# One-hot tables of a graph kernel: four groups of four tiles, one digit each, instead of one operation per digit and block

## What is computed

```python
x = ln(x + segsum(exp(-w)[:, None] * x[dst], src))              # layer 0: summed by src
x = ln(x + mlp(segsum(a32, src), segmax(a32, src), mean, u))    # layer 1: summed by src
x = ln(x + conv2(x, src, dst))                                  # layer 2: two convolutions, summed by dst
x = ln(x + attention(x, src, dst, a16))                         # layer 3: softmax over the edges of a dst
```

## Time and profile before

| | us |
|---|---|
| median of three runs | 9911.04 |
| profiled execution, its own time | 9915.06 |
| its span, first to last instruction | 9913.3 |
| src histogram loop (DVE, PE), with POOL's fetches beside it | 34.8 to 268.5 |
| POOL's last scatter of x | 351.1 |
| ranking, POOL's scatters | 383.6 to 2470.2 |
| everything behind the ranking | 2470.2 to 9913.3 |

### The profile page before, as it was taken

One profiled execution on the slowest core, in us unless ns is written; L12 is line 12 of the kernel. 1 busy time (PEld: TensorE's weight loads), 2 busy tenths in 40 slices (PEclk: granted clock), 3 DMA queues, 4 the chain that ended last, 5 costly groups with the idle time before them and its releaser, 6 DMA issues.

```text
span 9913.3 us, 48663 instructions
## 1 busy us (share of the span) xinstructions
PE 1598.8 (16%) x7747; PEld 1337.3 (13%) x7747; DVE 3662.5 (37%) x13931; ACT 2337.8 (24%) x3414; POOL 6882.5 (69%) x6983
## 2 busy tenths in 40 slices
PE   7544444442001400000000000000001000000000
PEld 6444444442000200000000000000001000000000
DVE  8666666663997411111111111111114222222225
ACT  0344444442000222222221222222220111111110
POOL 7677777777002577777777777777777777777776
PEclk7555555555555555555555555555555555555555
DMA  6445444443775122222221122222221222222221
GB/s 263 120 144 146 139 145 143 141 146 99 274 272 194 46 52 52 54 52 54 52 52 49 50 54 52 54 52 52 54 52 33 56 66 63 65 64 63 66 63 42
DMA packets 573559, 913.41 MB, mean 92 GB/s; under 512 B 335117, under 2 KB 351380, under 8 KB 547976
## 3 DMA queue, kind: packets, MB, share of 16 engines
q1 hardware_dynamic: 349752, 652.54, 19.6%
q0 software_dynamic: 223040, 258.35, 12.2%
q10 hardware_dynamic: 528, 0.15, 0.0%
HBM read 496.53 MB, written 414.02 MB: 92 GB/s over the span
## 4 chain that ended last, share of the span: by engine, by line
POOL 69%; issue 23%; DVE 7%; DMA 1%; PE 0%; ACT 0%; DVEq 0%; POOLq 0%; SPq 0%; ACTq 0%
POOL arena_a L673 45%; POOL by_src L621 16%; POOL arena_a L640 4%; DVE arena_a L1318 2%; DVE arena_a L1323 2%; POOL arena_a L590 1%; POOL x_at_start L600 1%; POOL adst_at_start L654 1%; PE banks L984 0%; DVE cap_blk L1281 0%; DVE cap_blk L1280 0%; DVE arena_b L1404 0%; DVE stat L1400 0%; DVE stat L1406 0%; PE banks L958 0%
## 5 line engine op out<-in xcount | busy, mean ns | idle before, releaser
L673 POOL DMA_INDIRECT arena_a<-table_c,decay x3136 | 2958.7, 943 | 1038.6 <-issue 955.1
L621 POOL DMA_INDIRECT by_src<-arena_b,idx_blk x1568 | 1609.0, 1026 | 506.6 <-issue 476.7
L673 POOL DMA_INDIRECT arena_a<-table_at,decay x1568 | 1489.6, 950 | 477.9 <-issue 477.9
L1530 DVE COPY banks<-arena_a 128x64 f32<-128x64 f32 x194 | 52.7, 271 | 3346.0 <-ACT banks L736 3346.0
L736 ACT ACTIVATE banks<-arena_a 128x1024 f32<-128x1024 f32 x196 | 369.6, 1886 | 2997.9 <-DMA arena_a<-table_c,decay 2997.9
L716 ACT ACTIVATE arena_b<-same_dst 128x1024 f32<-128x1024 f32 (+1 forms) x294 | 312.8, 1064 | 1701.3 <-DVE arena_a L1664 1569.2
L1213 DVE SCALAR_TENSOR_TENSOR arena_a<-arena_a,same_dst 128x64 f32<-128x64 f32 x1567 | 436.5, 279 | 709.5 <-DMA arena_a<-ids_rows 705.9
L932 PE MATMUL banks<-ident,chunk_end 128*64 128x128 f32 (+2 forms) x8 | 2.7, 443 | 3963.1 <-DVEq L1041 3963.1
L821 ACT ACTIVATE arena_b<-arena_a,decay 128x64 f32<-128x64 f32 x1568 | 384.8, 334 | 971.2 <-DMA by_src<-arena_b,idx_blk 864.2
L725 ACT ACTIVATE arena_a<-arena_a 128x1024 f32<-128x1024 f32 (+1 forms) x294 | 598.0, 2034 | 3.9 <-DVE arena_a L1664 2.0
L1215 DVE SCALAR_TENSOR_TENSOR arena_b<-arena_a,src_f,before 128x128 bf16<-128x128 f32 x1568 | 537.8, 343 | 0.0
(11 more groups left out here) (278 smaller groups left out, 4824.3 us busy)
## 6 DMA issues: line engine op xcount, KB each, us to landing
arena_a<-ids_rows SPq DMA_DIRECT2D x98, 1024.0 KB, 8.9
states_src<-arena_a SPq DMA_DIRECT2D x98, 1024.0 KB, 4.8
states_c<-arena_a SPq DMA_DIRECT2D x196, 512.0 KB, 2.6
hrows<-by_src SPq DMA_DIRECT2D x98, 776.0 KB, 6.1
states_at<-arena_a SPq DMA_DIRECT2D x98, 576.0 KB, 3.2
x_at_start<-arena_a SPq DMA_DIRECT2D x7, 7168.0 KB
arena_a<-x_at_start SPq DMA_DIRECT2D x98, 512.0 KB, 6.3
arena_a<-table_c,decay POOLq DMA_INDIRECT x3136, 2.4
```

The lines of the kernel that those rows point to most:

```text
L621: pool.indirect_dma_start(out=by_src, out_offset=AT(ap=idx_blk[r][:, k:k + 1], axis=0), in_=rows[r][:, k, :], in_offset=None)\
L673: pool.indirect_dma_start(out=gb[r][:, k * w:(k + 1) * w], out_offset=None, in_=table[g], in_offset=AT(ap=src_i[:, n * J + k:n * J + k + 1 ...
```

## The change

The two operations that make a block's one-hots, one for each digit, become eight: for each of the four groups of four tiles, one operation for `hi` (392 elements a partition) and one for `lo` (512). That holds for the sixteen tiles of the dst positions, for the histogram loop and for the ranking. In the ranking the order changes too: the groups of block n+1 are no longer made after `positions(n-1)`, but the first three after the selections `stage_b(n-1, 1)`, `(n-1, 2)` and `(n-1, 3)`, and the last after `positions(n-1)`. The wait for `hist_added` moves to the first of them. The number of elements written is the same.

```diff
-            def onehots(o, h, at):
-                v.tensor_tensor(oh_hi[h], in_groups(iota_hi), spread(digits[o, "hi"][:, at], HIGH), ALU.is_equal)
-                return v.tensor_tensor(oh_lo[h], in_groups(iota_lo), spread(digits[o, "lo"][:, at], LOW), ALU.is_equal)
+            def onehots_of_group(h, g, hi, lo):
+                for onehot, table, digit in ((oh_hi[h], iota_hi, hi), (oh_lo[h], iota_lo, lo)):
+                    ins = v.tensor_tensor(onehot[:, g], table, bf(digit[:, g * Q:(g + 1) * Q], table.shape[1]), ALU.is_equal)
+                return ins
+
+            def onehots(o, h, at):
+                for g in range(J // Q):
+                    ins = onehots_of_group(h, g, digits[o, "hi"][:, at], digits[o, "lo"][:, at])
+                return ins
...
-            def onehots_of(n):
...
+            def onehots_of(n, g):
+                at = slice(n * J, (n + 1) * J)
+                ins = onehots_of_group(n % 2, g, digits["src", "hi"][:, at], digits["src", "lo"][:, at])
+                if g == J // Q - 1:
+                    ins.then_inc(s("tile_onehots"), 1)
...
                     if n:
                         stage_b(n - 1, q)
+                    if n + 1 < NBLK and q:
+                        if q == 1:
+                            v.wait_ge(s("hist_added"), n + 1)
+                        onehots_of(n + 1, q - 1)
                 if n:
                     positions(n - 1)
                 if n + 1 < NBLK:
-                    v.wait_ge(s("hist_added"), n + 1)
-                    onehots_of(n + 1)
+                    onehots_of(n + 1, J // Q - 1)
```

More of the change, by code:

```diff
@@ L1190, in _ @@
                 of_nodes(o)
-            def onehots_of(n):
[L1194 to L1197, removed]
+            def onehots_of(n, g):
[3 more added lines that the diff above has]
+                    ins.then_inc(s("tile_onehots"), 1)
             v.wait_ge(s("onehots_used"), 2 * NB)
-            onehots_of(0)
+            for q in range(J // Q):
+                onehots_of(0, q)
             v.wait_ge(s("decay_ready"), 1)
```

## The result

The changed kernel takes 10067.45 us (median; 10058.97 to 10082.26), the kernel before 9912.12 us in the runs beside it: a ratio of 1.0158, 95% interval 1.0145 to 1.0172. It is 155 us slower where 78 us of gain were forecast. The profiled execution has a span of 10080.5 us against 9913.3. Going through the stages as in the earlier trace rows gives the difference of 167 us: the first scatter of the ranking comes 26.6 us later (forecast: 32 earlier), the ranking from its first scatter to the end of its last is 36.2 us shorter (forecast: 45), and 177 us are lost behind the ranking, 175 of them in a stage in which the change does nothing, the pass over the sorted rows on DVE (661 us before, 836 after). The three gather passes behind it are as long as before.

What follows compares the result with a forecast made beforehand. POOL's own work and issue were taken to bound the kernel, its DMAs held up by long one-hots. Startup -34, first block +2.3 and ranking -45 made -77 us: 9834 us, range 9808 to 9894.

Steps and rivals of the forecast that it cites:

- One small operation: DVE's one-hots: 0.277 and 0.340 us for 392 and 512 elements, a pair 0.617, a block 2.47 instead of 2.03.
- The first rival: Every small operation costs its whole duration, 0.80 us a pair; first ranking tile 25 us late, 9894 us; chance 0.11.
- the third: Histogram becomes the bound: small form streams at 1.1 ns an element, a pair 1.09 us; about 10,050 us; chance 0.07.
- the second: The ranking gains nothing, as four pairs catch as much as one block did; 9879 us; chance 0.12.
- the mean wait is the sum of the squared streaming times over twice the pair's time: POOL beside the histogram loop: 0.09 us mean wait, so a fetch costs 1.335 us and a scatter of x 1.37.
- 18 us wait for `node_index` 2: Startup: 49 scatters of x end at 234, `node_index` 2 comes at 252, so POOL waits 18 us, a new wait.
- The ranking: One-hots in eight pieces hold POOL up 16 us where 61 are measured; 45 us saved, range 25 to 61.
- longer hold: Ranking: shared ports held for a whole DVE instruction; eight pieces keep 45 us, gain 16 us, time 9862.
- Beside the rank counts: Ranking beside L1215: 31 of the scatters' 92 us extra time fall there and stay.
- The first block: Ranking's start: one whole set of one-hots and three groups stand ahead of the first `rows_ready`; 2.3 us later, once.
- Stages behind the ranking move earlier and keep their length: All stages after the ranking, the pass over the sorted rows included: start earlier, no change in length.
- the slower one: The rival in which the histogram becomes the bound: DVE ready at 499 instead of 362; about 10,050 us; chance 0.07.

Runs made afterwards that it cites:

- f1: Kernel before with only dst positions and histogram in small operations, a one-element memset ahead of each group's pair, the pass's loop at its old place; 0.9967.
- g1: Whole change plus a one-element memset ahead of each histogram group and 45 memsets restoring the pass's loop place; 9847.04 us, 0.9932 to the kernel before.
- f3: Kernel before with a second long `lo` operation in each block of histogram and dst positions, slower by construction; no total given, POOL's DMAs there at most 2.04 us.
- c1: Kernel before with only the ranking changed to eight small operations between the selections, the pass's loop at its old place; 0.9972 to the kernel before.
- f5: Kernel before with only dst positions and histogram in small operations, one memset a block, loop at its old place; no total given, ranking begins at 348.71.
- f2: Kernel before with only dst positions and histogram changed, to four operations a block of eight tiles and one digit, loop at its old place; 0.9984.
- f4: Kernel before with only the ranking in small operations, all eight in one row behind the positions, loop at its old place; 1.0018 to the kernel before.

## Why the prediction was wrong, point by point

**One small operation: right.** 0.617 us a pair was forecast, 0.61 came, and with it the loop: 293 us for its end (299 forecast), the second table at 248 (252). The first rival, 0.80 a pair, and the third, a histogram that becomes the bound, are out, and by the ranking so is the second.

**"... the mean wait is the sum of the squared streaming times over twice the pair's time": the first step that failed.** It holds that a request waits for the operation that it meets and for no more, as the earlier trace rows showed for operations of 0.98 and 1.22 us. For a row of 0.35 and 0.41 us it fell to both sides. The fetches lost 0.02 instead of 0.09 us: POOL's 0.95 + 0.30 = 1.25 us is about two pairs (1.22), and a `hi` operation stretches from 0.35 to 0.38 where POOL comes in (39.16 above), so that the two keep in step; that this stretching is what keeps them so is argued, not tested, and that the fetches came out better than forecast was luck. The scatters, at 0.98 + 0.30, fell out of step and took 4.56 us. By the formula they take 1.07; at 1.852 the 98 of them cost 77 us more. The 18 us wait for `node_index` 2 did not appear, since POOL was late itself; in f1 and g1, where the scatters are short, it did (23.4 and 24.3 us). The startup thus ended 26.6 us late instead of 32 early.

By the Trainium skill ("SBUF — State Buffer", section "SBUF: two separate sides") the pair of ports that DVE and GpSimd share is an exclusive lock: whichever starts first has it for the whole instruction, and the other is blocked. That a request waits for an end agrees with f3; that it can miss eleven ends in a row and get in at the twelfth (4.56 - 0.98 us, one end every 0.30) goes beyond that section, and there the measurement decides.

**The ranking: right in mechanism and sign, 36 of 45 us.** The prediction put what one-hots cost POOL at 16 us. Picked in the same way, 163 of POOL's requests meet a small `lo` operation and lose 24.1 us, 0.15 each; 113 meet a `hi` and lose 0.2 us in all. That is 24 us where the formula gave 16 and the prediction's longer hold 45. Beside the rank counts (L1222, before L1215) 27 us are lost, where 31 were put down. The first block cost some 2 us (c1 begins the ranking 2.4 later than before; 2.3 forecast).

**"Stages behind the ranking move earlier and keep their length": the second step that failed, and the larger.** Nothing in the pass was touched, but its loop stood at another place of DVE's program, and the pass took 175 us more. The prediction costed the added instructions by what they do, and not by what stands behind them. The earlier trace rows hold nothing of it, since before the loop fits; the page's count of instruction packets and the order of DVE's program would have been the views to ask.

**The rivals.** None named either cause; the slower one came to the right sign, with 10,050 near the measured 10,067, by a mechanism that did not occur. What stays open: what decides whether POOL gets in at the end of a small operation, and why a request that has missed one gets in at one end of the histogram's iteration alone. It is not the lack of a gap (f3), not the memset as an opening (f5), and not the DMA side (f1).

## What to carry to other kernels

When a change adds or removes instructions ahead of a long hardware loop on the same engine (here one of 282), ask where the loop will lie: its time moved by 6 to 8 us a turn with nothing in it changed, and 85 idle instructions put it back. When work on one engine is cut into short pieces to let another in, put other work between the pieces; a long even row of them can shut the other out for longer than one large piece did. A stage that a change doesn't touch should be looked at in the trace of after before its length is taken as given.

## What the runs showed of the hardware

- A hardware loop of 282 instructions on DVE costs 6 to 8 us more in every turn when it begins at 112 or 130 modulo 256, with five instruction packets of 8192 bytes a turn, and nothing at 140, 172 or 214.
- An indirect DMA of POOL that takes 0.98 us alone mostly takes 4.56 us beside an even row of DVE operations of 0.35 and 0.41 us (22 of 31 take over 4.5), and 0.98 to 1.5 when a memset of 0.06 us stands ahead of every pair or of every fourth pair. Beside operations of 0.55 to 0.7 us with few gaps (f2), or of 0.97 to 1.23 us with none (f3), it loses no more than the rest of one.
- Such a DMA that has missed the end of a small operation got in at the end of a block's last one: at the end of the row in the ranking (f4, 68 of 68), at the end of the iteration's first block in the histogram (23 of 25).
